# A decoder layer: half of the memory products formed in the key stage, moments of x in the value stage, memory outputs every second step from step 5

## Reference

```python
def attn(hidden_states, Wq, bq, ..., Wo, M, z):        # H=32 heads, HKV=8, D=128, G=4
    q = (hidden_states @ Wq.T + bq).reshape(b, s, H, D)
    sig_q = elu(q) + 1.0
    q_sel = sig_q[:, :, ::G, :]
    num = einsum('bshd,hde->bshe', q_sel, M)
    den = einsum('bshd,hd->bsh', q_sel, z)[..., None] + 1e-6
    out_heads = repeat(num / den, G, axis=2)
    return out_heads.reshape(b, s, H * D) @ Wo.T

x = x + attn(layernorm(x), ...)
x = x + xattn(layernorm(x), ctx, ...)      # 32 heads over 4 key/value heads; keys and values of ctx and x
x = x + ffn(layernorm(x), ...)             # router softmax, top 8 of 64 expert biases
```

## Time and profile before

| | |
|---|---|
| median of 3 runs | 743.04 us (742.65 to 750.49) |
| the profiled execution's own time | 745.13 us |
| its span | 743.0 us |
| PE busy, share of the span | 720.2 us, 97% |
| DVE busy | 417.1 us, 56% |
| ACT busy | 352.8 us, 47% |
| POOL busy | 44.6 us, 6% |
| mean granted clock of the matmul engine | 0.993 |

### The profile page before, as it was taken

One profiled execution on the slowest core, in us unless ns is written; L12 is line 12 of the kernel. 1 busy time (PEld: TensorE's weight loads), 2 busy tenths in 40 slices (PEclk: granted clock), 3 DMA queues, 4 the chain that ended last, 5 costly groups with the idle time before them and its releaser, 6 DMA issues.

```text
span 743.0 us, 10784 instructions
## 1 busy us (share of the span) xinstructions
PE 720.2 (97%) x3644; PEld 597.9 (80%) x3644; DVE 417.1 (56%) x914; ACT 352.8 (47%) x1033; POOL 44.6 (6%) x47
## 2 busy tenths in 40 slices
PE   7998899999999999999999999999999999999996
PEld 5886678888888788888888888888888888888873
DVE  2475997676312445554464455364555446567885
ACT  3443685543323545444464454364544455444641
POOL 0026620000000000000000000000000000000000
PEclk9999999999999999999999999999999999999998
DMA  9757530003333041120041110013111001001001
GB/s 337 279 157 251 184 123 1 0 9 134 113 117 126 20 158 43 44 57 15 22 160 41 48 49 14 21 34 136 42 50 49 14 21 37 15 1 47 18 30 42
DMA packets 48545, 56.83 MB, mean 76 GB/s; under 512 B 3200, under 2 KB 29824, under 8 KB 48512
## 3 DMA queue, kind: packets, MB, share of 16 engines
q1 hardware_dynamic: 43904, 48.02, 20.1%
q10 hardware_dynamic: 4608, 8.39, 3.0%
HBM read 45.91 MB, written 10.49 MB: 76 GB/s over the span
## 4 chain that ended last, share of the span: by engine, by line
PE 90%; DVE 6%; DMA 1%; ACT 1%; issue 1%; SPq 0%; POOL 0%; ACTq 0%; DVEq 0%
PE bank L683 24%; PE bank L662 23%; PE bank L497 14%; PE bank L760 7%; PE bank L630 6%; PE bank L818 6%; PE bank L796 4%; PE bank L488 2%; PE bank L525 1%; PE bank L741 1%; DVE sig L1202 1%; DMA keys_dram<-kvout 1%; PE bank L722 1%; PE bank L571 1%; DVE kvout L1186 1%
## 5 line engine op out<-in xcount | busy, mean ns | idle before, releaser
L662 PE MATMUL bank<-xnT,regA 128*128 128x512 f32 x768 | 190.5, 398 | 0.0
L683 PE MATMUL bank<-regC,oT 128*128 128x512 f32 x768 | 180.0, 390 | 1.4 <-DVE oT L1106 1.4
L683 PEld LDWEIGHTS bank<-regC,oT 128*128 128x128 f32 x768 | 143.8, 188 | 31.5 <-DVE oT L1106 1.8
L662 PEld LDWEIGHTS bank<-xnT,regA 128*128 128x128 f32 x768 | 140.1, 188 | 28.6 <-issue 0.8
L1033 ACT ACTIVATE probs<-bank,negmax 128x128 f32<-128x128 f32 x256 | 89.8, 377 | 50.1 <-DVE negmax L1321 50.1
L1106 DVE TENSOR_TENSOR oT<-bank,oT 128x512 fp32r<-128x512 f32 x64 | 44.1, 691 | 71.1 <-ACT oT L845 70.9
L845 ACT CAST pT<-bank 128x512 fp32r<-128x512 f32 x64 | 34.5, 589 | 93.1 <-PE bank L796 93.1
L863 ACT ACTIVATE qT<-bank 128x512 f32<-128x512 f32 x64 | 39.3, 614 | 74.4 <-PE bank L662 74.3
L497 PE MATMUL bank<-regC,xnT 128*128 128x512 f32 x288 | 70.7, 397 | 0.0
L760 PEld LDWEIGHTS bank<-k_ring,qT 128*128 128x128 f32 x512 | 62.0, 191 | 3.7 <-ACT qT L863 1.1
L760 PE MATMUL bank<-k_ring,qT 128*128 128x128 f32 x512 | 62.4, 275 | 0.7 <-ACT qT L863 0.7
(11 more groups left out here) (110 smaller groups left out, 802.7 us busy)
## 6 DMA issues: line engine op xcount, KB each, us to landing
raw<-in_L_attn_Wo SPq DMA_DIRECT2D x8, 1024.0 KB, 5.7
raw<-in_L_xattn_Wo SPq DMA_DIRECT2D x4, 2048.0 KB, 9.3
wq_raw<-in_L_xattn_Wq SPq DMA_DIRECT2D x16, 512.0 KB, 4.3
k_ring<-keys_dram SPq DMA_DIRECT2D x32, 128.0 KB, 2.3
v_raw<-vals_dram SPq DMA_DIRECT2D x64, 64.0 KB, 2.3
rawk<-in_L_xattn_Wv SPq DMA_DIRECT2D x4, 512.0 KB, 4.0
rawk<-in_L_xattn_Wk SPq DMA_DIRECT2D x4, 512.0 KB, 8.2
resid<-in_x SPq DMA_DIRECT2D x4, 512.0 KB, 11.2
```

Of the source, the lines that this page charges most:

```text
L662: last = nc.tensor.matmul(k_bank[:, :], wq[:, a, head, c, :], xnT[:, b, c, half * HALF:(half + 1) * HALF], start=i == 0, stop=i == 3 * KC - 1)
L683: last = nc.tensor.matmul(bank[7][:, :], oT[:, parity, a, h, :], wo[:, b, h, :], start=h == 0 and i == 0, stop=h == GH - 1 and i == 2)
```

## The change

Heads 0 to 3 get their memory product in the key stage: iteration i has the product of head i-3 and the transposes for head i-2. Heads 4 to 7 follow in steps 0 to 4 of the memory stage. For that the folds on POOL, the loads of Wo on SP and the second load of M move forward, the loads of the bias and z rows move behind five Wo loads, and the banks are given out anew (products in banks 4 and 7, early M and Wo transposes in banks 5 and 6, x in 0, Wq in 1). The moments of the x tiles are taken four at a time: those of tiles 0 to 3 in the value stage ahead of the split of the key weights, those of 4 to 7 after the first two norms, each group with one root on POOL. The memory outputs stand in steps 5, 6, 8, 10, 12, 14 and 16, and output 7 behind the steps; the latent transposes follow one output later, and the last two stand ahead of output 7 and behind latent value 1. Counts of matmuls and transposes stay as they are. The diff, cut to its core (on ACT the helpers `memory_weights` and `memory_rows` are called at the same places):

```diff
-        TR_CTX, TR_X, TR_MEM, TR_X2 = 0, 8, 24, 40
-        MM_VCTX, MM_KCTX, MM_MEM, MM_VLAT, MM_KLAT, MM_XQ = 0, 8, 16, 40, 48, 56
-
-        def tr_x(t):
-
-            return TR_X + t if t < 2 else TR_X + 2 * (t - 1)
-
-        def tr_wqa(m):
-
-            return tr_x(m + 2) + 1 if m < MH - 2 else tr_x(NT - 1) + m - (MH - 4)
-
-        def tr_mem(m):
-
-            return TR_MEM + 2 * m
-
-        def mm_query(i):
-
-            return MM_MEM + (max(2 * i - 1, 0) if i <= MH else MH + i)
-
-        def mm_memwo(m):
-
-            return MM_MEM + 2 * m + 2
+        EARLY = MH // 2
+        tr_order = [("ctx", t) for t in range(NT)] + [("x", 0)]
+        for i in range(NT):
+            tr_order += [("x", i + 1)] if i + 1 < NT else []
+            tr_order += [("wqa", i - 1)] if i else []
+            tr_order += [("wqa", i)] if i == NT - 1 else []
+            tr_order += [("mem", i - 2), ("wo", i - 2)] if 0 <= i - 2 < EARLY else []
+        tr_order += [(kind, m) for m in range(EARLY, MH) for kind in ("mem", "wo")]
+        tr_order += [("latent", t) for t in range(NT)]
+
+        mm_order = [("vctx", t) for t in range(NT)]
+        for i in range(NT):
+            mm_order += [("memwo", i - 3)] if 0 <= i - 3 < EARLY else []
+            mm_order += [("kctx", i)]
+        for i in range(2 * NT):
+            mm_order += [("query", i)]
+            mm_order += [("memwo", i + EARLY - 1)] if 1 <= i <= MH - EARLY else []
+        mm_order += [("vlat", t) for t in range(NT)] + [("klat", i) for i in range(NT)] + [("xq", h) for h in range(GH)]
+
+        def tr(kind, i):
+            return tr_order.index((kind, i))
+
+        def mm(kind, i):
+            return mm_order.index((kind, i))
 
         def mm_act_count(k):
 
-            in_memory = min(max((k - MM_MEM) // 2, 0), MH)
-            return min(k + 1, MM_MEM) + in_memory + max(k + 1 - MM_VLAT, 0)
+            return sum(kind != "query" for kind, _ in mm_order[:k + 1])
 
         def mm_dve_count(k):
 
-            return min(max(k + 1 - MM_MEM, 0), MM_VLAT - MM_MEM)
+            return sum(kind in ("query", "memwo") for kind, _ in mm_order[:k + 1])
...
         def tr_bank(k):
-            return bank[k % 2]
+            kind, i = tr_order[k]
+            if kind in ("mem", "wo"):
+                return bank[(5, 6)[kind == "wo"]] if i < EARLY else bank[kind == "wo"]
+            if kind in ("ctx", "latent"):
+                return bank[i % 2]
+            return bank[kind == "wqa"] if (kind, i) != ("wqa", NT - 1) else bank[0]
 
         def mm_bank(k):
-
-            if k in [mm_query(i) for i in range(0, MH, 2)]:
-                return bank[7]
-            return bank[2 + k % 2]
+            kind, i = mm_order[k]
+            if kind == "memwo":
+                return bank[4] if i % 2 else bank[7]
+            return bank[2 + i % 2]
...
         def outputs_in(i):
 
-            return {MH + 1: (0,), MH + 3: (1,), MH + 5: (2,), MH + 7: (3,), MH + 8: (4,), MH + 9: (5,)}.get(i, ())
+            return {5: (0,), 6: (1,), 8: (2,), 10: (3,), 12: (4,), 14: (5,), 16: (6,)}.get(i, ())
...
-            sp.wait_ge(tr_done, TR_CTX + NT)
+            sp.wait_ge(tr_done, tr("ctx", NT - 1) + 1)
             for m in range(MH):
-                if m == 2:
-                    sp.wait_ge(tr_done, tr_wqa(3) + 1)
+                if m == 5:
+                    sp.wait_ge(tr_done, tr("wqa", 3) + 1)
                     sp.dma_start(bq_all, bq_heads.broadcast_to([P, MH, P])).then_inc(rows_loaded, 16)
                     sp.dma_start(z_all, attn_z.rearrange("(a m) n -> a m n", a=1).broadcast_to([P, MH, P]))\
                       .then_inc(rows_loaded, 16)
+                    sp.wait_ge(tr_done, tr("mem", EARLY - 1) + 1)
+                    sp.dma_start(mem[:, :, :], mem_heads[:, MH // 2:MH, :]).then_inc(mem_loaded, 16)
                 if m >= 2:
                     sp.wait_ge(fold_done, m - 1)
                 sp.dma_start(woa_raw[:, m % 2, :, :, :].rearrange("p o g n -> p o (g n)"),
                              woa_heads[m]).then_inc(woa_loaded[m % 2], 16)
-                if m == 6:
-                    sp.wait_ge(tr_done, tr_mem(3) + 1)
-                    sp.dma_start(mem[:, :, :], mem_heads[:, MH // 2:MH, :]).then_inc(mem_loaded, 16)
...
-            for t in range(NT):
-                root(t)
+            for r in range(2):
+                pool.wait_ge(var_ready, r + 1)
+                nc.gpsimd.tensor_tensor(x_rstd[:, 4 * r:4 * r + 4], x_vareps[:, 4 * r:4 * r + 4], neg_half[:, :],
+                                        ALU.pow).then_inc(rstd_ready, 1)
...
+                if 0 <= i - 3 < EARLY:
+                    memory_weights(i - 3)
+                if 0 <= i - 2 < EARLY:
+                    memory_transposes(i - 2)
+                    wo_transposes(i - 2)
+                keys(mm("kctx", i), wkv1, ctxT, i // KV, i % KV)
...
-                if 1 <= i <= MH:
-                    memory_weights(i - 1)
-                if i < MH:
-                    memory_transposes(i)
+                if 1 <= i <= MH - EARLY:
+                    memory_weights(i + EARLY - 1)
+                if i < MH - EARLY:
+                    memory_transposes(i + EARLY)
...
             for i in range(2 * NT + 2):
                 memory_step(i)
-            for t in range(6, NT):
-                memory_output(t)
-                latent_transposes(t - 2)
+            latent_transposes(NT - 2)
+            memory_output(NT - 1)
 
             pe.wait_ge(wkv_lo, 3 * KC)
             for t in range(4):
-                values(MM_VLAT + t, wkv2, xnT, t)
-                if t in (0, 3):
-                    latent_transposes(6 + t // 3)
+                values(mm("vlat", t), wkv2, xnT, t)
+                if t == 1:
+                    latent_transposes(NT - 1)
...
+            def x_moments(r):
+
+                for t in range(4 * r, 4 * r + 4):
+                    if t % 2 == 0:
+                        dve.wait_ge(x_loaded[t // 2], 16)
+                    last = nc.vector.bn_stats(x_stats[:, t, :], resid[:, t, :])
+                settled(last)
+                for t in range(4 * r, 4 * r + 4):
+                    last = nc.vector.bn_aggr(x_meanvar[:, t, :], x_stats[:, t, :])
+                settled(last)
+                nc.vector.tensor_scalar(x_vareps[:, 4 * r:4 * r + 4], x_meanvar[:, 4 * r:4 * r + 4, 1], LN_EPS, None,
+                                        ALU.add).then_inc(var_ready, 1)
+
+            def norm_x(t):
+                dve.wait_ge(rstd_ready, t // 4 + 1)
+                if t >= 2:
+                    dve.wait_ge(tr_done, tr("x", t - 2) + 1)
+                nc.vector.tensor_scalar(xn[:, t % 2, :], resid[:, t, :], x_meanvar[:, t, 0:1], x_rstd[:, t:t + 1],
+                                        ALU.subtract, ALU.mult).then_inc(xn_ready, 1)
+
+            x_moments(0)
...
             norm_x(0)
             norm_x(1)
+            x_moments(1)
             for i in range(NT):
+                if i == 0:
+                    x_low(tr("x", 0), 0)
                 if i + 2 < NT:
                     norm_x(i + 2)
-                if i == 0:
-                    x_low(tr_x(0), 0)
                 if i + 1 < NT:
-                    x_low(tr_x(i + 1), i + 1)
+                    x_low(tr("x", i + 1), i + 1)
                 if i:
                     memory_wq(i - 1)
                 if i == NT - 1:
                     memory_wq(i)
+                if 0 <= i - 3 < EARLY:
+                    memory_weights(i - 3)
+                if 0 <= i - 2 < EARLY:
+                    memory_rows(i - 2)
...
                 memory_step(i)
                 for t in outputs_in(i):
                     add_memory(t)
-                    if 1 <= t <= 4:
-                        x_low(TR_X2 + t - 1, t - 1)
-            for t in range(6, NT):
-                add_memory(t)
-                x_low(TR_X2 + t - 2, t - 2)
-                wkv_low(t - 6, wkv2, (t - 4) * KC)
-            for t in range(6, NT):
-                x_low(TR_X2 + t, t)
+                    if t:
+                        x_low(tr("latent", t - 1), t - 1)
+            x_low(tr("latent", NT - 2), NT - 2)
+            wkv_low(0, wkv2, 2 * KC)
+            add_memory(NT - 1)
+            wkv_low(1, wkv2, 3 * KC)
+            x_low(tr("latent", NT - 1), NT - 1)
 
```

More of the change, by code:

```diff
@@ L120, in decoder_layer @@
         kvout = sb("kvout", [P, 2, D], F, first)
+        x_stats = sb("x_stats", [P, NT, 6], F, first)
+        x_meanvar = sb("x_meanvar", [P, NT, 2], F, first)
+        x_vareps = sb("x_vareps", [P, NT], F, first)
+        x_rstd = sb("x_rstd", [P, NT], F, first)
         first.close()
@@ L459, in _ @@
                 if m >= 2:
-                    pool.wait_ge(tr_done, tr_mem(m - 2) + 2)
+                    pool.wait_ge(tr_done, tr("wo", m - 2) + 1)
                 nc.gpsimd.tensor_tensor(wofold[:, m % 2, :, :], w[:, :, 0, :], w[:, :, 1, :], ALU.add)\
                     .then_inc(fold_done, 1)
```

(9 more changed lines are left out.)

173 lines of the change are left out of this document (89 added, 84 removed).

## The result

| | before | after |
|---|---|---|
| median | 742.97 us (4 runs) | 767.39 us (765.5 to 769.05, 4 runs) |
| ratio | | 1.031 (95% interval 1.028 to 1.034) |
| profiled execution: own time, span | 745.13, 743.0 us | 769.05, 767.0 us |
| PE busy | 720.2 us | 731.4 us |
| mean granted clock | 0.993 | 0.974 |

The forecast was 753.4 us with a range to 757.5. The direction was right and the place was right; the size was not.

A forecast was written before the change was run, and what follows sets the result against it. The prediction took the matmul engine to bound the kernel, so that only its waits could change. Parts 1 to 4 summed as -4.8 + 1.2 + 9.75 + 4.3 = +10.4 us on the 743.04 median: 753.4 us, range 744.5 to 757.5.

The forecast's parts named there:

- rival 3: Clock falls to 1.2 GHz in the tail and some output pairs, fold 2 late: +13 to +16 us; chance 0.10.
- Part 3: Memory stage: outputs 2 to 6 each wait 1.95 us for a sigT low from VectorE, 9.75 us in all.
- Part 1: Memory stage, half the products moved out: later product waits go, 4.8 us won; the first, 2.5 us, stays.
- coin on its edge: Memory stage's first wait: POOL's fold at 2.1 us or VectorE's L1202 at 2.2 first; VectorE first wins 3.7 us.
- shared port: VectorE and POOL sharing in proportion, no exclusive lock: first wait about 1.5 us shorter, sum +8.9 instead of +10.4.
- Part 2: Key stage: matmul engine waits 1.8 us for the first fold, a 0.64 us x transpose wait goes: +1.2 us.
- Part 4: End of memory stage: waits of 1.4, 2.0 and 0.8 us up to output 7, 4.3 us in sum.
- Rival 1: Head's stalls go: VectorE comes before POOL and the fold is in time; +4.9, 747.9 us; chance 0.22.
- Rival 2: Memory stage: outputs don't wait, the odd half's low is in time; 733.5 to 743.7 us; chance 0.13.

The follow-up runs named there:

- Experiment 9: Changed kernel with matmuls that nobody reads ahead of nearly every memory-stage wait, the x tile's bank wait left open: 757.2 us (1.017).
- experiment 2: Changed kernel with memory outputs 1 to 6 one step later: 746.9 us (1.0024).
- experiment 5: Changed kernel with VectorE's residual sum, norm and latent split of outputs 0 to 5 one memory step later: 761.15 us (1.021).
- experiment 7: best0 with the loads of bias and z rows and M's second half behind the sixth Wo load instead of the fifth: 740.26 us (0.9935).
- best0: Changed kernel with the outputs' schedule as before the change and x tile 1 in bank 1: 738.26 us (0.9911), once more 739.6 us (0.9935).
- experiment 1: Changed kernel with x tile 1 transposed into bank 1 instead of bank 0: 761.4 us (1.021).
- experiment 10: Changed kernel with VectorE's residual sums and norms of outputs 1 to 5 one step later and x tile 1 in bank 1: 751.7 us (1.0085).
- experiment 4: Changed kernel with seven matmuls that nobody reads ahead of the wait of each of outputs 2 to 6: 762.4 us (1.023).

## Why the prediction was wrong

**The clock (the step that failed).** The working priced each wait at its own length and let the clock out of it: "if the clock falls here as after 71.4, it costs up to 1.5 us more; it did not fall after the 2.53 us at 92.54, so I take nothing and keep 1.5", and for the pairs it stood in rival 3 only, with a chance of 0.10. One fall in four gaps of over 1 us is what before had shown, and the change made ten gaps of 0.97 us or more where there had been four, five of them at regular distance. Measured: 30 us more at the 1.2 GHz level, about 10 us of time. Experiment 9 shows it as cause: the same waits without the gaps are 7 to 11 us cheaper. The trace of before shows 1.5 us for one gap of four, about 0.4 us each, so zero was not what it says. But that price would not have been enough: six more gaps at 0.4 us make 2.3 us and 755.7 in all. The ten gaps of the kernel after cost about 12 us of slow matmuls (10.6 and the 1.5 of before), 1.2 each, and this no row of before could give.

The Trainium skill (TensorE: Matmul & The Clock Gate, HAM oscillation — how this bites in real kernels) describes a kernel whose engine falls to the lower clock again and again because of repeated waits, and pays half of the slow time on top of the waits. The traces here agree in kind: after, stretches at 0.5 begin behind waits of 1.9 us, each behind 12 us of dense work, and are absent where the same waits are filled. They differ in size: in the kernel of the Trainium skill the waits are 3 to 5 us long and every block behind them is slow, while here 1.9 us were enough, and only behind a part of the waits. The remedy of the Trainium skill is an order of the loops in which the engine works longer before it has to wait; experiment 2 is of the same kind, an order in which the waits of the outputs are gone.

**Part 3, the output waits.** The mechanism and its size held: 1.90, 1.89, 1.86 and 1.89 us where 1.95 was forecast, by VectorE's chain, and experiment 5 took it down to 0.33 by moving nothing but the residual sum, the norm and the latent split on VectorE. But "outputs 2, 3, 4, 5 and 6 have this form" was wrong for output 6. Its step is 16, queries end with step 15, and so 2.76 us of cover were missing: 4.62 us. Sum 12.2 instead of 9.75.

**Part 1, the head.** The waits of the later products are gone, as forecast. The first one did not stay at 2.5; it became 0.97 and the next product's 2.91. POOL's fold 7 came later than my sum had it, because its block of weights was still on the way, and met the denominators of step 1 (the first L1241 took 2.48 us from 79.60, POOL's first half ran from 79.54) instead of L1202's successor. 3.9 us where I had 2.5. VectorE's timeline (kernel after), the denominators' first and second instruction:

```profile
79.60 2.48 DVE L1241 SCALAR_TENSOR_TENSOR kvout<-sig,rawk 128x128 f32<-128x128 f32 x1
...
82.02 0.28 DVE L1241 SCALAR_TENSOR_TENSOR kvout<-sig,rawk 128x128 f32<-128x128 f32 x1
```

The "coin on its edge" was more than two-sided: with folds 5 to 7 in other places (experiment 7) the sum of both waits was 3.3 us, and 1.8 in best0. That a port is held for a whole instruction was right: the first row ends at 82.08, just behind POOL's half at 81.94; the next one takes 0.28, and the third, begun at 82.23 inside POOL's second half (82.02 to 83.46), again 1.37. Which instruction it hits cannot be summed to tenths of a microsecond. The price that the prediction gives a shared port is off: twice 0.69 is 1.38, so L1202 would have been 0.96 us shorter, not 1.5, and the sum +9.4 instead of +8.9.

**Part 2, the fold's date.** The wait of 1.8 us for fold 0 did not come. The weights were issued at 30.80, 1.4 us later than in before where I had 2.5, and had landed at 38.94, 8.1 us behind that instead of 9.3. The stage as a whole began 0.75 us earlier. (From the prediction's own terms the wait is 45.0 - 43.33 = 1.7 us, not 1.8.) POOL (kernel after):

```profile
38.94 2.37 POOL L467 TENSOR_TENSOR raw<-raw 128x1024 f32<-128x1024 f32 x1 [4.11 <-DMA raw<-in_L_attn_Wo]
41.39 1.28 POOL L472 TENSOR_TENSOR wofold<-raw 128x512 f32<-128x512 f32 x1
```

Fold 0 is ready at 42.7, and in the key stage of before the place was at 43.33, or 42.6 with a stage that begins 0.75 us earlier. The kernel after came there at 46.08, held up by the bank wait. In experiment 1, without the bank wait, 0.18 us appear there, in experiment 10 0.40: the date is just met. So the lower bound that I had given (0) was the true value for the kernel after, and nearly so without the bank wait. In its place came a wait of 2.05 us that I had not seen, at 36.61, for bank 0 (experiment 1), with 1.5 us of slow clock. The 0.64 us of the earlier trace rows went as forecast.

**Part 4, the end.** 1.41 and 1.83 us where I had 1.4 and 2.0. The third wait of 0.8 is hidden by the slow clock in the kernel after; with the clock up it is 0.54 (experiment 9, in front of 191.48 where the row shows it). The clock fell here, which was the 1.5 us that I had kept aside: 7.86 instead of 5.60 us for output 7, 2.3 us.

**The sum.** Waits forecast +10.4, measured +13.4 (outputs +2.4, head +1.4, bank +2.05, fold -1.8, end -1.1). Clock forecast 0, measured +10.6 with the 1.3 us of slower outputs behind a wait in it. The waits alone would have made 756.4, inside the range; the term that took the time out of it is the clock.

**The rivals.** Rival 3 named the mechanism and gave 756 to 759, with a chance of 0.10. It was the nearest and too small: there were six slow stretches, in the rows at 37.00, 86.36, 125.37, 156.03, 186.71 and 200.69, and some were longer than one output (0.59 on average over the 7.6 us from 86.3 makes (1 - 0.59) x 7.6 x 2 = 6.2 us at the lower level). Rival 1 was right for the fold, which cost nothing, and wrong for the head with its 3.9 us. Rival 2 is out, since the outputs wait; its lowest value, -9.5, is all that can be won, while its own terms add up to -9.1.

## What to carry to other kernels

A wait of the matmul engine costs more than its length once waits come regularly: look in the trace for one fall of the clock behind a gap, and charge every new gap at least a share of it; here that share would still have been a third of the true price. When work is put one step earlier, read from the trace when its last operand is ready relative to the step that it moves to, for each step by itself; the last one, where the loop's cover has run out, is another case. And when a change gives out banks anew, go through the holders one after the other: two tiles in a row in one bank are a wait.

## What the runs showed of the hardware

Extra matmuls in the gaps made a kernel faster: seven of them (1.78 us) in each gap of 1.9 us left outputs 2 to 5 at 5.86 or 5.87 us and none at 7.4 (experiment 4), and with nearly every gap filled the kernel took 757.2 us against 764.55 beside it. The falls of the clock differ between executions of one and the same kernel (outputs 2, 4, 6 and 7 slow in one profile, 2, 3, 5, 6 and 7 in another, 4, 6 and 7 in the third), while the waits in front of outputs 2 to 5 agree to 0.05 us. Of the 16 outputs behind a wait of 1.86 to 1.90 us in four profiles (the changed kernel three times and experiment 1), nine took 7.4 us or more; behind the wait of 4.6 us it was four of four. Of the 16 outputs behind a gap of 0.24 to 0.33 us (outputs 2 to 5 of experiments 4, 5, 9 and 10) none did. A gap of about 3 us in front of output 6 was followed by 7.41 and 7.42 us (2.99 us in experiment 4, 3.06 in 5) and by 5.85 (3.07 in 10). Why a gap of 1.9 us is followed by a fall in one place and not in the next stays open.
